# A transformer-like block on one Trainium2 core: routing tables built in pieces, and the first routed tile turned between two down products

## The reference, cut to what matters

```
x = hidden_states.reshape(-1, 256)
shared_out = silu_and_mul(x @ shared_gate_up) @ shared_down
router_logits = x @ gate_w                         # 8 experts
topk_w, topk_i = lax.top_k(softmax(router_logits), 2)
topk_w = topk_w / sum(topk_w)
combine = sum(one_hot(topk_i, 8) * topk_w[..., None], axis=1)
for each expert e:                                 # 256 -> 512 -> 256
    moe_out += combine[:, e:e+1] * (silu_and_mul(x @ w_gate_up[e]) @ w_down[e])
out = moe_out + shared_out
```

## Time and profile before

| | |
|---|---|
| median of 3 runs | 1432.47 us (1432.46 to 1432.76) |
| the profiled execution | 1434.49 us |
| its span, first to last instruction | 1432.8 us |
| PE busy | 1334.9 us (93%) |
| DVE, ACT, POOL busy | 925.9, 756.2, 686.2 us |
| mean granted TensorE clock | 0.969 |
| the shared expert and its routing | about 500 to 675 us of the span |
| the routed stage | about 675 to 1050 us |

### The profile page before, as it was taken

One profiled execution on the slowest core, in us unless ns is written; L12 is line 12 of the kernel. 1 busy time (PEld: TensorE's weight loads), 2 busy tenths in 40 slices (PEclk: granted clock), 3 DMA queues, 4 the chain that ended last, 5 costly groups with the idle time before them and its releaser, 6 DMA issues. The chain is left out here.

```text
span 1432.8 us, 31669 instructions
## 1 busy us (share of the span) xinstructions
PE 1334.9 (93%) x9954; PEld 1017.8 (71%) x9955; DVE 925.9 (65%) x1689; ACT 756.2 (53%) x1461; POOL 686.2 (48%) x853
## 2 busy tenths in 40 slices
PE   4899999999999589998998999999987999999998
PEld 3555555555555268887877888888876788888887
DVE  7799999999997278766554333333335766665553
ACT  0477777777778544432342333333426656665642
POOL 7577777777772156443675223310044554445210
PEclk9999999999999789999999999999976999999999
DMA  3222222222221122114732333241131110111000
GB/s 103 79 81 83 79 88 82 73 86 85 78 73 38 51 83 80 60 59 138 238 124 82 97 97 95 67 142 51 45 96 41 30 44 28 34 45 30 15 16 30
DMA packets 85891, 105.53 MB, mean 74 GB/s; under 512 B 11249, under 2 KB 76145, under 8 KB 85425
## 3 DMA queue, kind: packets, MB, share of 16 engines
q1 hardware_dynamic: 75344, 70.38, 15.5%
q0 software_dynamic: 10464, 34.09, 7.5%
HBM read 53.05 MB, written 23.99 MB: 54 GB/s over the span
## 5 line engine op out<-in xcount | busy, mean ns | idle before, releaser
L469 ACT ACTIVATE e_t<-st_ps 128x512 f32<-128x512 f32 x512 | 278.5, 597 | 105.5 <-PE st_ps L557 101.9
L407 DVE TENSOR_REDUCE row_max<-s_ps 128x4 f32<-128x1024 f32 x256 | 311.3, 1218 | 21.8 <-PE s_ps L562 19.5
L584 PE MATMUL o_ps<-e_t,v_st 128*32 128x256 f32 x2048 | 166.5, 398 | 0.1
L557 PE MATMUL st_ps<-q_st,k_st 32*128 32x256 f32 x1024 | 160.5, 333 | 6.2 <-DMA q_st<-m_rows 3.6
L562 PE MATMUL s_ps<-k_st,q_st 32*128 32x256 f32 x1024 | 158.1, 342 | 5.1 <-DVE row_max L407 3.5
L557 PEld LDWEIGHTS st_ps<-q_st,k_st 32*128 32x128 f32 x1024 | 106.1, 187 | 56.0 <-issue 36.3
L1773 POOL DMA_INDIRECT gathered_tail<-sorted_results,result_at x64 | 70.8, 1106 | 125.3 <-POOLq L2299 107.2
L1640 PE MATMUL y_ps_moe<-w_all_moe,xt_hi_moe 128*128 x568 | 116.5, 286 | 7.7 <-DVE xt_lo_moe L1440 7.7
L2039 DVE TENSOR_TENSOR h_all_tail<-silu_tail,u_ps_tail 128x512 f32<-128x512 f32 x64 | 43.8, 685 | 118.7 <-ACT silu_tail L1888 64.5
L1446 DVE TENSOR_TENSOR h_all_moe<-silu_moe,u_ps_moe 128x512 f32<-128x512 f32 x71 | 48.8, 687 | 109.3 <-PE u_ps_moe L1609 109.3
L1124 ACT COPY y_sb_moe<-y_ps_moe 128x256 f32<-128x256 f32 x71 | 26.5, 373 | 162.2 <-PE y_ps_moe L1640 162.2
(11 more groups left out here) (341 smaller groups left out, 3613.7 us busy)
## 6 DMA issues: line engine op xcount, KB each, us to landing
k_st<-k_part SPq DMA_DIRECT2D x96, 128.0 KB, 2.1
q_st<-q_part SPq DMA_DIRECT2D x96, 128.0 KB
stage_moe<-in_experts POOLq DMA_DIRECT2D x21, 512.0 KB, 4.2
rows_in_moe<-sorted_rows SPq DMA_DIRECT2D x71, 128.0 KB, 2.0
sorted_results<-y_sb_moe SPq DMA_DIRECT2D x71, 128.0 KB, 1.7
c_in<-in_ctx SPq DMA_DIRECT2D x32, 128.0 KB, 2.2
x_sb<-in_x SPq DMA_DIRECT2D x32, 128.0 KB, 2.1
xn_moe<-in_ctx SPq DMA_DIRECT2D x8, 512.0 KB, 4.4
```

The source lines that it names most:

```text
L407: nc.vector.tensor_reduce(out, s_ps[p % 2][:], AX_X, ALU.max).then_inc(s["max_taken"], 1)
L469: nc.scalar.activation(e_t[t % 4][:, b, :, :], st_ps[:, b, :, :], ACT.Exp, scale=float(DH) ** -0.5)\
L557: last = nc.tensor.matmul(out, w, moving, start=True, stop=True)
L584: last = nc.tensor.matmul(o_ps[32 * j:32 * j + 32, :], values[:, at:at + 32], e_t[(2 * u + j // 2) % 4][:, j % 2, half_, :], start=(half_ ...
```

## The change

DVE's `find_weights` is cut in two: `find_turns` (its first ten operations) stays between chunk 2 and chunk 3 of group 15, the rest runs behind the last `low`, ahead of tile 0's low part. The last `add` moves from before step -1 into it, behind tile 0's low part. `move_rows` is cut into four parts that run in steps 0, 12, 13 and 14. PE's transposes of tile n+1 become a function `turn_rows`; that of tile 0 now stands between `down(15, 2)` and `down(15, 3)`, ahead of the wait for `weights_found`, and so no longer behind the last down product. The first count of `r2["down_done"]` moves from tile 0's first transpose to tile 1's.

```diff
--- before.py
+++ after.py
@@ -1287,7 +1287,7 @@
                 nc.vector.scalar_tensor_tensor(out=tab[:, ROW, :], in0=expert[:], scalar=float(REGION), in1=before[:],
                                                op0=ALU.mult, op1=ALU.add).then_inc(s["rows_found"], 1)
 
-            def find_weights():
+            def find_turns():
 
 
 
@@ -1305,6 +1305,9 @@
                 then(nc.vector.scalar_tensor_tensor(out=past[:, 0:ROUTER, :], in0=turn_of[:].unsqueeze(1).to_broadcast(by_place),
                                                     scalar=0.0, in1=const("turn").unsqueeze(2).to_broadcast(by_place),
                                                     op0=ALU.add, op1=ALU.is_equal))
+
+            def find_weights():
+
                 nc.vector.tensor_scalar(last_use[:], end[:], end[:, ROUTER - 1:ROUTER], float(NT), ALU.is_ge, ALU.mult)
                 then(nc.vector.tensor_tensor(before[:], before[:], expert[:], ALU.add))
                 nc.vector.tensor_tensor(last_use[:], last_use[:], end[:], ALU.max)
@@ -1327,9 +1330,15 @@
                 then(nc.vector.scalar_tensor_tensor(out=start[:], in0=start[:], scalar=float(P), in1=const("first_row"),
                                                     op0=ALU.mult, op1=ALU.subtract))
                 nc.vector.tensor_tensor(moved[:], row_all[:], start[:].unsqueeze(1).to_broadcast(wide), ALU.add)
+
+            def mark_rows():
                 then(nc.vector.tensor_scalar(row_all[:], row_all[:], 0.0, None, ALU.is_gt))
+
+            def keep_moved():
                 then(nc.vector.scalar_tensor_tensor(out=moved[:], in0=moved[:], scalar=1.0, in1=row_all[:],
                                                     op0=ALU.add, op1=ALU.mult))
+
+            def find_results():
                 nc.vector.tensor_reduce(both[:, 0, :], moved[:], AX_X, ALU.max)
                 then(nc.vector.tensor_reduce(both_sum[:], moved[:], AX_X, ALU.add))
                 then(nc.vector.tensor_tensor(both[:, 1, :], both_sum[:], both[:, 0, :], ALU.subtract))
@@ -1422,19 +1431,21 @@
                     if m == 2 and g + 2 < GROUPS:
                         low_of(g + 2)
                     if m == 2 and g + 1 == GROUPS:
-                        find_weights()
+                        find_turns()
                     if m == 2 and g + 3 < GROUPS:
                         stats_of(g + 3)
                 low(CHUNKS - 1)
                 if g + 1 < GROUPS:
                     slots_of(g + 1)
-            add(GROUPS - 1)
+            find_weights()
 
             def body(n, c, i):
                 if there(n, 1):
                     dve.wait_ge(r2["hi_taken"], n + 2)
                     nc.vector.tensor_tensor(t_lo[(c + 1) % 2], t_ps[0][:, 0:D], t_hi[(c + 1) % 2].bitcast(F32),
                                             ALU.subtract).then_inc(r2["lo_taken"], 1)
+                if isinstance(n, int) and n == -1:
+                    add(GROUPS - 1)
                 if there(n, -1):
                     dve.wait_ge(r2["h_high"], n)
                     nc.vector.tensor_tensor(ht_lo, t_ps[1][:], ht_hi.bitcast(F32), ALU.subtract)\
@@ -1464,8 +1475,14 @@
                     weigh()
                 if isinstance(n, int) and n == 11:
                     spread()
+                if isinstance(n, int) and n == 0:
+                    move_rows()
+                if isinstance(n, int) and n == 12:
+                    mark_rows()
                 if isinstance(n, int) and n == 13:
-                    move_rows()
+                    keep_moved()
+                if isinstance(n, int) and n == 14:
+                    find_results()
 
             ring_steps(dve, body)
 
@@ -1565,8 +1582,26 @@
                         down(g, m - 2)
                 if g + 2 < GROUPS:
                     make_wide(g + 2)
-            for m in (2, 3):
-                down(GROUPS - 1, m)
+            def turn_rows(n, c, i):
+
+                pe.wait_ge(rows_loaded[(c + 1) % 4], 16 * uses(c, i, 1))
+                wait_count(pe, r2["lo_taken"], n + 1)
+                if isinstance(n, int) and n == 10:
+                    pe.wait_ge(pooling["shifted_done"], 1)
+                if isinstance(n, int) and n == 12:
+                    pe.wait_ge(pooling["spread"], 1)
+                if turning(n):
+                    pe.wait_ge(r2["rotated_low"], turning(n))
+                for kc in range(2):
+                    last = nc.tensor.transpose(t_ps[0][:, kc * P:(kc + 1) * P],
+                                               rows_in[(c + 1) % 4][:, kc * P:(kc + 1) * P], ident[:])
+                    if kc == 0 and isinstance(n, int) and n == 0:
+                        last.then_inc(r2["down_done"], 1)
+                last.then_inc(r2["turned"], 1)
+
+            down(GROUPS - 1, 2)
+            turn_rows(-1, -1, 0)
+            down(GROUPS - 1, 3)
 
             pe.wait_ge(s["weights_found"], 1)
             pe.wait_ge(s["product_done"], CHUNKS * GROUPS)
@@ -1575,21 +1610,8 @@
                 if there(n, 0):
                     where = looked_up(pe, WHERE, n, 0, 2 * SLOT)
                     pieces = looked_up(pe, NEED, n, 6, PIECES)
-                if there(n, 1):
-                    pe.wait_ge(rows_loaded[(c + 1) % 4], 16 * uses(c, i, 1))
-                    wait_count(pe, r2["lo_taken"], n + 1)
-                    if isinstance(n, int) and n == 10:
-                        pe.wait_ge(pooling["shifted_done"], 1)
-                    if isinstance(n, int) and n == 12:
-                        pe.wait_ge(pooling["spread"], 1)
-                    if turning(n):
-                        pe.wait_ge(r2["rotated_low"], turning(n))
-                    for kc in range(2):
-                        last = nc.tensor.transpose(t_ps[0][:, kc * P:(kc + 1) * P],
-                                                   rows_in[(c + 1) % 4][:, kc * P:(kc + 1) * P], ident[:])
-                        if kc == 0 and isinstance(n, int) and n == -1:
-                            last.then_inc(r2["down_done"], 1)
-                    last.then_inc(r2["turned"], 1)
+                if there(n, 1) and not (isinstance(n, int) and n == -1):
+                    turn_rows(n, c, i)
                 if there(n, -1):
                     pe.wait_ge(r2["product_done"], n)
                     wait_count(pe, r2["h_low"], n - 1)
```

## The result

The changed kernel took 1421.47 us in the median of 4 runs (1418.44 to 1423.32), beside 1432.59 for the kernel before (4 runs): 11.1 us less, a ratio of 0.9918 with a 95% interval of 0.9903 to 0.9934. Forecast were 1420.6, in a range of 1418.5 to 1426.5. The profiled execution took 1421.25 us; its span is 1419.6, its mean granted clock 0.972.

What follows compares the result with a forecast made beforehand. PE, busy 93% of the span, was taken as the bound, so only its idle or slow-clocked time pays. Seam 3.8 plus steps 12 to 14 8.1 gave 11.9 us, from 1432.47 to 1420.6, range 1418.5 to 1426.5.

Steps and rivals of the forecast that it cites:

- The seam: Between the two stages: first routed product at 673.6 instead of 677.39, saving 3.8 us, bounds 3.0 to 5.0.
- the gap of about 1.5: Sign on PE ahead of tile 1's transposes: one gap of about 1.5 us, ended by the table reads.
- The rows for tile 0: At the seam: their load lands at 669.4, over 0.7 us before PE needs it, so no wait.
- Step 0: start and moved behind tile 0's multiply, 0.2 + 0.42 us, mostly finding POOL idle: cost nothing, cover gone 1 us.
- Steps 12 to 14: move_rows' parts there remove 5.77 us of PE idle and 2.34 of slow clock: 8.1 us saved, bounds 7.3 to 8.3.
- a job may last 2.9 us for nothing: Steps 12 to 14: an odd job on DVE up to 2.9 us long costs PE nothing.
- Rival 1: POOL late for weigh in step 10: at worst 5.7 us lost, 1426.3 us; chance 0.12.
- 5.1 of slack stays: Argument against POOL being late for weigh: it loses 6.0 us of its 11.1 us wait for the eighth sum.
- Rivals 2 to 5: Seam gives nothing, 1424.4, 0.06; only seam pays, 1428.7, 0.03; doubled POOL waits, 1439.2, 0.02; nothing changes, 1432.5, 0.02.
- Rival 4: Steps 12 to 14: blocked operations wait for two POOL instructions in turn, losing 18.6 us, 1439.2 us; chance 0.02.

Runs made afterwards that it cites:

- early_signal: Changed kernel, but PE's table reads wait only for DVE's write of the second table, not the end of find_weights: 1421.2 us, ratio 0.9918.
- parts_only: Kernel before with its old seam, only move_rows cut into four parts: 1424.33 us, ratio 0.9945.
- turn_late: Changed kernel, but tile 0's rows are turned behind the last down product: 1422.4 us, ratio 0.9932.
- whole_late: Changed kernel, but all of move_rows runs in step 67, where POOL is idle: 1421.92 us, ratio 0.9926.
- two_in_one: Changed kernel, but mark_rows and keep_moved both run in step 12: 1424.69 us, ratio 0.9938.
- after_again: The changed kernel, unaltered, run and profiled once more: 1422.44 us, ratio 0.9931.
- after: The changed kernel's first runs and profile: median 1421.47 us, profiled execution 1421.25 us.
- seam_only: Changed kernel, but with move_rows whole in step 13: 1428.39 us, ratio 0.9976.
- low_waits: Changed kernel, but POOL starts the second w_lo split only after weigh's multiply: 1423.08 us, ratio 0.9934.
- parts_again: One more profile of the kernel with the old seam and move_rows in four parts: execution of 1424.07 us.

## Why the prediction was right, point by point

**The seam: right in size, right in what ends it.** Forecast 3.8 us, measured 3.77. Chunk 3's multiply, find_weights' later end, the reads as the last to end, and the gap of about 1.5 (1.21) all came as worked out; early_signal shows the reads by taking 0.94 us of them away. The forecast named the clock as part of what is removed, and parts_only gives its share: against parts_only, where the clock held, the seam is worth 8.6 - 6.35 = 2.25, so some 1.5 of the 3.77 was slow clock. So the old seam's low clock, which the forecast took as given, is not fixed by its gap: without it the seam would have been worth 2.25. That figure rests on two profiles of each kernel. The rows for tile 0 were there in time: no gap stands ahead of its transposes. That the early turn has no gain of its own, the prediction did not say; turn_late shows it.

**Step 0: right.** start and moved ran at 0.16 and 0.42 us with POOL idle.

**Steps 12 to 14: right in mechanism, 0.6 us too much.** Forecast 8.1, measured 7.54. The parts kept their waits (2.14 and 2.19 us) and no down product of PE waited for them. The term that was mis-sized is "a job may last 2.9 us for nothing": tiles 12 to 16 take 20.36 where whole_late, with no parts there, takes 19.91, so 0.45 is left; and 19.91 itself is 0.3 above four pitches of 4.90. The 2.9 is right as the point where PE begins to wait for the low part, 3.0 in two_in_one. But two jobs of 1.7 us cost nothing and two of 2.1 to 2.4 us already cost 0.45 to 0.66: the forecast counted the low part's slack and not the cover of PE's table reads, in whose place the small "issue" gaps stand. That the reads cause them is argued, not tested.

**Rival 1, POOL late for weigh: it happened, at part of its price.** It was given a chance of 0.12 as a case apart. In fact every profile with the new seam and POOL's order as it was, but turn_late, has the multiply above its 1.45 (1.57 to 3.15; the kernel before itself had 1.67 once). Tiles 9 to 12 are 0.2 to 0.9 us longer than the 18.55 of before in five of them, 1.3 in early_signal, where the clock fell to 0.78 in the next step, and 3.4 in after_again against a forecast worst of 5.7. In two_in_one it is the clock, 0.76, more than the multiply. The step that failed was "5.1 of slack stays": POOL's own slack was there (it waited 6.2 us for the sum), but the weights it had asked for before that wait landed 0.8 (after) to 1.8 us (after_again) later than it could use them. Why they landed late was not tested. This term, forecast as nothing, and the 0.6 above make up the difference between 11.9 and the 10.6 that the stages give.

**The time.** 1432.47 - 10.6 would be 1421.9; the three sets of runs of the changed kernel gave 1421.47, 1422.44 and 1423.83, the forecast was 1420.6. All three medians lie above the forecast, by 0.9 to 3.2, as the missing 1.3 us would have it. The profiled execution lies below its own forecast, 1421.25 for 1422.6, and that is luck: its attention ended 2.5 us sooner.

**Rivals 2 to 5** did not come: the seam paid (seam_only), step 13's gain was not taken back (parts_only), no stage shows a doubled wait in the changed kernel, and both idle gaps were not due all the same. Rival 4's mechanism, one job blocked twice, is seen in low_waits, 1.40 and 2.44 us in a row; it cost 2 us there, far from the 18.6 that the rival needed.

## What to carry to other kernels

When a small VectorE operation lasts over a microsecond, look at what GpSimd does at that moment before cutting the work up: moving it whole to where GpSimd is idle did as much as spreading it. Size the slack of a pipeline stage once, for every engine's work that hides in it (here PE waited for data from 3.0 us a tile on, but 2.1 us already cost something), and judge each odd job with its worst wait against the smaller figure. And when a stage is pulled forward, list what loses slack by it on the other engines, with the landing times of their loads: the seam's 3.8 us went with 0.7 more in tiles 9 to 12 here, and with 3.4 in another profile of the same kernel.

## What the runs showed of the hardware

- A 128x8 operation lasted 0.16 us with GpSimd idle and 1.83 beside its rotation; a 128x256 one 0.29 and 2.48; the multiply in weigh 0.42 and 3.15. The reductions of 128x256 (0.41 to 0.42) never grew. The Trainium skill says in SBUF — State Buffer, "Who interferes with whom", that an operation with two SBUF inputs, or one in a two-port mode, waits for GpSimd's instruction and a reduction never does. The rows above agree.
- PE's sequencer needs 1.4 to 1.5 us for its first two table reads. It is free while the array has queued work. At the new seam it showed as a gap of 1.21 us named "issue"; gaps of 0.64 to 0.74 with that name stand behind the waits of weigh in most profiles, and there the reads as cause are argued and not tested.
- The same idle gap of 2.0 us was followed by a granted clock of 0.74 to 0.76 over the next stretch in two profiles and by 1.00 in two others. In weigh, 1.23 us in parts_only was followed by 0.76 and 1.24 in parts_again by 1.00, and 2.04 in after by 1.00. One of 1.1 us in two_in_one left it at 1.00.
- The attention, the same code in all kernels, ended at 480.4 to 485.6 us. With a scatter of some 5 us in the runs, differences below 2 us were told here only by cutting the traces into stages.
